# Half-row tiles for three convolutions, no copied outer rows, and two later stages further behind

## The reference

```python
x = x + L0(gn(x))   # 5 Newton-Schulz steps for the inverse of each 128x128 matrix
x = x + L1(gn(x))   # 3x3 convolution of activations rounded to whole numbers of up to 127,
                    # integer weights, scale and bias; the scale comes from the largest |gn(x)| of the batch
x = x + L2(gn(x))   # 5x5 convolution whose kernel is zero off its diagonal
x = x + L3(gn(x))   # 3x3 circular convolution (written with FFTs)
```

## Time and profile before

| | us |
|---|---|
| median of 3 runs | 4041.86 (4040.77 to 4042.82) |
| the profiled execution | 4042.99 |
| its span | 4041.2 |
| TensorE busy, VectorE busy | 3882.1, 3161.3 |
| ScalarE busy, GpSimd busy | 2458.9, 2416.6 |

### The profile page before, as it was taken

How to read it: one execution, slowest core, us unless ns; L and a number is a source line. 1 busy time by engine, 2 the same in 40 slices (tenths; PEclk the granted TensorE clock), 3 DMA queues, 4 the chain that set the end, 5 groups by cost and what they waited for, 6 DMA issues and landing times. The chain is left out here.

```text
span 4041.2 us, 91064 instructions
## 1 busy us (share of the span) xinstructions
PE 3882.1 (96%) x35017; PEld 2994.3 (74%) x35017; DVE 3161.3 (78%) x7205; ACT 2458.9 (61%) x4490; POOL 2416.6 (60%) x3154
## 2 busy tenths in 40 slices
PE   7999999999999999999999589999999999999998
PEld 7999999999999999999999344444444444444443
DVE  5888888888888888888888667777777777777774
ACT  5776677777777777777777345455455455555552
POOL 6888888888888888888888323333332332332332
PEclk9999999999999999999999799999999999999999
DMA  2122211222122222221221368777777777778774
GB/s 71 56 63 64 64 59 59 64 64 59 58 64 64 64 64 64 64 64 56 61 64 43 75 133 175 174 165 162 164 168 175 169 160 163 169 171 175 162 159 106
DMA packets 339918, 422.11 MB, mean 104 GB/s; under 512 B 25312, under 2 KB 288160, under 8 KB 323104
## 3 DMA queue, kind: packets, MB, share of 16 engines
q1 hardware_dynamic: 324128, 377.40, 39.1%
q10 hardware_dynamic: 15360, 38.88, 3.7%
HBM read 135.18 MB, written 134.22 MB: 67 GB/s over the span
## 5 line engine op out<-in xcount | busy, mean ns | idle before, releaser
L1228 POOL TENSOR_TENSOR xn<-F,xn 128x512 f16<-128x512 f32 x512 | 543.4, 1093 | 1189.6 <-ACT xn L1270 1189.6
L1444 PE MATMUL bank<-xn,wt 128*128 128x512 f16 (+1 forms) x3072 | 765.0, 384 | 15.3 <-DVE xn L1314 11.8
L484 ACT ACTIVATE P<-bank 128x512 f32<-128x512 f32 x1024 | 606.6, 608 | 267.6 <-PE bank L1007 155.4
L1466 PE MATMUL bank<-xk,wt 128*32 128x512 f16 x6144 | 634.9, 386 | 43.3 <-DMA xk<-xn 42.9
L1328 DVE SCALAR_TENSOR_TENSOR x<-bank,wu,x 128x512 f32<-128x512 f32 x512 | 377.4, 747 | 299.7 <-PE bank L1471 269.9
L1444 PEld LDWEIGHTS bank<-xn,wt 128*128 128x128 f16 (+1 forms) x3072 | 296.0, 102 | 361.8 <-issue 40.1
L1267 ACT ACTIVATE F<-x,nb,r 128x2048 f32<-128x2048 f32 x128 | 268.1, 2095 | 346.6 <-issue 218.6
L1471 PE MATMUL bank<-xk,wth 128*32 128x512 f16 x3072 | 469.2, 381 | 0.0
L1466 PEld LDWEIGHTS bank<-xk,wt 128*32 128x32 f16 x6144 | 295.6, 95 | 204.9 <-DMA xk<-xn 47.6
L334 POOL TENSOR_TENSOR W<-W 128x512 f16<-128x512 f32 x256 | 289.5, 1160 | 145.1 <-ACT W L517 145.1
L1338 DVE BATCH_NORM_STATS2 bs<-x 128x6 f32<-128x512 f32 x512 | 355.5, 694 | 17.6
(11 more groups left out here) (144 smaller groups left out, 8369.3 us busy)
## 6 DMA issues: line engine op xcount, KB each, us to landing
xk<-xn SPq DMA_DIRECT2D x512, 131.8 KB, 4.4
X<-in_x SPq DMA_DIRECT2D x64, 1024.0 KB, 4.8
x_scratch<-X SPq DMA_DIRECT2D x64, 1024.0 KB, 5.8
X<-x_scratch SPq DMA_DIRECT2D x64, 1024.0 KB, 8.6
out<-x SPq DMA_DIRECT2D x64, 1024.0 KB, 6.8
xh<-xn SPq DMA_DIRECT2D x192, 131.8 KB, 4.6
xh<-xn ACTq DMA_DIRECT2D x192, 131.8 KB, 5.5
xh<-xn SPq DMA_DIRECT2D x192, 65.9 KB, 5.2
```

Of the source, the lines that this page charges most:

```text
L484: nc.scalar.activation(into[:, 4 * q:4 * q + 4, :], banks[q][:, :].rearrange("p (m w) -> p m w", m=4), ACT.Copy).then_inc(sb, 1)
L1228: ins = nc.gpsimd.tensor_tensor(padded(xn[l][n % 2], 1)[:, a + 1:a + 5, L:L + H], F[l][:, a:a + 4, :], padded(xn[l][n % 2], 0)[:, a + 1:a ...
L1444: nc.tensor.matmul(bank, wt[l][:, a, k, :], v, start=(k == a == b == 0), stop=False)
L1466: nc.tensor.matmul(bank[32 * q:32 * q + 32, :], wt[2][:, a, e, 32 * q:32 * q + 32], rows(b, 2 * q + e, 0), start=(a == b == e == 0), stop= ...
```

## The change

- `LATE` becomes (None, 0, 2, 4): layer 2 of image `s - 2`, layer 3 of image `s - 4`; the means and variances of layer 3 are those of image `s - 3`. The pipeline has one step more. Layer 2's x has three buffers (was two).
- Every convolution is cut into strips of 64 rows by 32 columns: four strips (the column groups) on the upper 64 rows of the array, four on the lower. Outer rows are read in place: the upper half's strip of column group 0 in the band below, or the lower half's of group 3 in the band above, as the tables `back` say, with weights `wth` laid over the same partitions and columns. `xh`, its 12 DMAs an image, and ScalarE's waits for them are gone.
- TensorE's stream interleaves: after each four upper strips of one piece come four lower strips of an earlier piece, in another PSUM bank. Lower strips follow one to three pieces behind, and are brought up to date (`finish`) before a mean or variance that needs them.
- `xk` is written in two passes, high part after `high` and low part after `normed`, 16 DMAs of half the size; SyncE first waits until layer 2 of image `s - 2` is done.
- On ScalarE `wrap` comes after `upper` of layer 2. `var(2, s)` on TensorE comes after the first piece of layer 2 instead of after the last of layer 3.
- Weights: `whf[1]`, `whf[3]` become 128 x 3 x 128 (were 96 x 128), are zeroed by GpSimd and filled by 6 small DMAs each; scaling and splitting cover the larger tiles. SyncE waits for those zeros.

The core of the diff:

```diff
-        outer = (None, 6 * C, H, 6 * C)
+        edges = (None, [(row, d + 1, o) for row, d, o in HALO1], [(row, 0, o) for row, _, o in HALO2],
+                 [(row, d + 1, o) for row, d, o in HALO1])
+        planes = (None, 3, 1, 3)
...
-                    for l, rows in ((1, w1h), (3, w3h)):
-                        sp.dma_start(whf[l][:, :], rows).then_inc(w_loaded, 16)
-                    sp.wait_ge(ones_set, 4)
-                    for k, (row, _, o) in enumerate(HALO2):
-                        r = row % RB
-                        sp.dma_start(whf[2][C * r:C * r + C, C * o:C * o + C],
-                                     w2h[C * k:C * k + C, C * o:C * o + C]).then_inc(w_loaded, 16)
+                    sp.wait_ge(ones_set, 6)
+                    for l, rows in ((1, w1h), (2, w2h), (3, w3h)):
+                        for k, (row, plane, o) in enumerate(edges[l]):
+                            r = row % RB
+                            sp.dma_start(whf[l][C * r:C * r + C, plane, C * o:C * o + C],
+                                         rows[C * k:C * k + C, C * o:C * o + C]).then_inc(w_loaded, 16)
...
-            LATE = (None, 0, 1, 3)
+            GAP = BEHIND = 2
+            LATE = (None, 0, 2, 4)
...
+            products = (None, [(0, 0)], [(0, 0), (0, 1), (1, 0)], [(0, 0), (0, 1), (1, 0)])
+            length = [None] + [len(products[l]) * mats[l] for l in (1, 2, 3)]
...
-                    sp.wait_ge(normed[1], 1)
-                    halo_copies(sp, 1, 0, False)
                     sp.wait_ge(xk_zeroed, 2)
                     for s in range(STEPS):
-                        if there(s - 1):
-                            sp.wait_ge(normed[2], s)
-                            for r in range(RB):
-                                skew_row(sp, r, s - 1)
+                        two, mid, three = images_of(s)
                         if there(s + 2):
                             load(s + 2)
-                        if there(s + 1):
-                            sp.wait_ge(normed[1], s + 2)
-                            halo_copies(sp, 1, s + 1, False)
-                        if there(s - 3):
-                            store(s - 3)
-                        if there(s - 2):
-                            sp.wait_ge(wrapped, 2 * (s - 1))
-                            halo_copies(sp, 3, s - 2, False)
+                        if there(three):
+                            store(three)
+                        if there(s):
+                            need(sp, conv_ps[2], BPI * (s - 1))
+                            sp.wait_ge(high[2], s + 1)
+                            skew(s, 0)
+                            sp.wait_ge(normed[2], s + 1)
+                            skew(s, 1)
...
-                        if there(s - 2):
-                            wrap(s - 2)
-                            act.wait_ge(wrapped, 2 * (s - 1))
-                            halo_copies(act, 3, s - 2, True)
                         if there(s):
                             upper(2, s)
+                        if there(mid):
+                            wrap(mid)
...
+                    def strips(l, n, u, half, i):
+                        a, b = products[l][i // mats[l]]
+                        k = i % mats[l]
+                        if half == 0 and i == 0:
+                            if u == 0:
+                                ready(l, n)
+                            bank_free(l, n, u)
+                        bank = bank_of(l, n, u)
+                        part = slice(64 * half, 64 * half + 64)
+                        for q in range(4):
+                            back = {(1, 0): -1, (0, 3): 1}.get((half, q), 0)
+                            cols_ = slice(32 * q, 32 * q + 32)
+                            w = (wth if back else wt)[l][part, a, k, cols_]
+                            if l == 2:
+                                at = (4 * u + 1) * PW + L + SK - (2 * q + k) + back * (PW + RB)
+                                v = xk[n % 2][part, b, at:at + 4 * PW].rearrange("p (j w) -> p j w", w=PW)[:, :, 0:H]
+                            else:
+                                at = 4 * u + 1 + back
+                                v = padded(xn[l][n % 2], b)[part, at:at + 4, L + k - 1:L + k - 1 + H]
+                            ins = nc.tensor.matmul(bank[cols_, :], w, v, start=(half == i == 0),
+                                                   stop=(half == 1 and i == length[l] - 1))
...
+                    def piece(l, n, u):
+                        k = place[l, n, u]
+                        for i in range(length[l]):
+                            strips(l, n, u, 0, i)
+                            if below[0] < k - (i < GAP):
+                                lower_strips()
+                        while below[0] < k - BEHIND:
+                            lower_strips()
...
                     for s in range(STEPS):
+                        two, mid, three = images_of(s)
+                        for u in range(BPI):
+                            if there(s):
+                                piece(1, s, u)
+                        if there(mid):
+                            mean(3, mid)
+                        for u in range(BPI):
+                            if there(three):
+                                piece(3, three, u)
+                            if there(mid) and u == 0:
+                                if there(s):
+                                    finish(1, s, BPI - 2)
+                                var(3, mid)
+                            if there(s) and u == 1:
+                                mean(2, s)
+                        for u in range(BPI):
+                            if there(two):
+                                piece(2, two, u)
+                            if there(s) and u == 0:
+                                if there(three):
+                                    finish(3, three, 0)
+                                var(2, s)
+                    finish(*order[-1])
```

More of the change, by code:

```diff
@@ L1115, in conv_net @@
             THIRD = 3
-            xs = [None, x1s] + [[sb(f"x{l}_{n}", [H, NJ, H]) for n in range(k)] for l, k in ((2, 2), (3, THIRD))]
+            xs = [None, x1s] + [[sb(f"x{l}_{n}", [H, NJ, H]) for n in range(k)] for l, k in ((2, THIRD), (3, THIRD))]
             T = sb("T", [H, NJ, H])
-            xh = [None] + [None if l == 2 else [sb(f"xh{l}_{n}", [6 * C, parts[l], NJ * PW], kinds[l]) for n in range(2)]
-                           for l in (1, 2, 3)]
             xk = [sb(f"xk{n}", [H, 2, SFLAT], f16) for n in range(2)]
@@ L1141, in conv_net @@
             wrap_chain = sem("wrap_chain")
-            halo = [None] + [[sem(f"halo{l}_{n}") for n in range(2)] for l in (1, 2, 3)]
-            skewed = halo[2]
+            skewed = [sem(f"skewed{n}") for n in range(2)]
             xk_zeroed = sem("xk_zeroed")
+            upper_ps = sem("upper_ps")
             conv_ps = [None] + [sem(f"conv_ps{l}") for l in (1, 2, 3)]
@@ L1386, in _ @@
                     for s in range(STEPS):
+                        two, mid, three = images_of(s)
                         for u in range(BPI):
-                            if u == BPI - 1 and there(s - 2):
-                                deviations(3, s - 2)
+                            if u == BPI - 1 and there(mid):
+                                deviations(3, mid)
                             if there(s):
@@ L1435, in conv @@
                                 pe.wait_ge(wrapped, 2 * n + 2)
-                        bank_free(l, n, u)
-                        products = [(0, 0)] if l == 1 else [(0, 0), (0, 1), (1, 0)]
-                        for k in range(taps[l]):
-                            at = L + k - taps[l] // 2
-                            for a, b in products:
-                                v = padded(xn[l][n % 2], b)[:, 4 * u + 1:4 * u + 5, at:at + H]
-                                nc.tensor.matmul(bank, wt[l][:, a, k, :], v, start=(k == a == b == 0), stop=False)
@@ L1484, in var, with lower_strips @@
                                          stop=True).then_inc(gvar[l], 1)
-                    for s in range(STEPS):
-                        if there(s):
-                            for u in range(BPI):
-                                conv(1, s, u)
-                        if there(s - 2):
-                            mean(3, s - 2)
+                    below = [0, 0]
+                    def lower_strips():
+                        k, i = below
+                        if i == 0:
+                            pe.wait_ge(upper_ps, k + 1)
+                        strips(*order[k], 1, i)
+                        below[:] = [k, i + 1] if i + 1 < length[order[k][0]] else [k + 1, 0]
@@ new lines, in piece, with finish @@
+                    def piece(l, n, u):
[6 more added lines that the diff above has]
+                            lower_strips()
+                    def finish(l, n, u):
+                        k = place[l, n, u]
```

(4 more changed lines are left out.)

128 lines of the change are left out of this document (47 added, 81 removed).

## The result

The changed kernel takes 3908.39 us (median of 4 runs, 3891.88 to 3914.69) against 4042.34 for the kernel before: a ratio of 0.9663 (95% interval 0.9632 to 0.9693), 134 us less. The forecast was 3725. The direction came true and the time lies in the range, but less than half of the gain is there. The profiled execution took 3911.49 us, 1.8 more than its span.

What follows compares the result with a forecast made beforehand. Prediction: TensorE bounds the old kernel at 26.44 us a step; afterwards VectorE's loop does at 21.9. Ends of 2433 + 59 x 21.9 = 3725 us, range 3670 to 3990.

Steps and rivals of the forecast that it cites:

- Tiles on TensorE: TensorE's convolutions: 74 turns a step at 0.218 us, 16.1 us, with upper and lower strips running at once.
- small products: TensorE's four products for means and variances: 0.5 us each with the array emptying either side, 1.9 us a step.
- Halves take turns: Rival, 20% together with slow issue: row halves do not overlap, 144 turns, 33.3 us a step, 4398 us.
- weight loads are exposed: Rival, 6%: 0.10 us of weight load shows in each TensorE turn, 25.4 us a step, 3932 us.
- side sum: Claim that halves taking turns decides once overlap is worth less than a third of the lower strips.
- VectorE's loop: VectorE as next bound: 12.0 + 9.7 = 21.7 us a step, including a wait for ScalarE's root; bounds 21.5 to 22.6.
- keeping up: Check that the other engines are in time for VectorE; TensorE's variance of layer 2 had 1.7 us of slack.
- a - 1.4: Time 1.4 us before a, the end of VectorE's part A, when TensorE passes layer 3's variance.
- The clock: Rival, 10%: TensorE idles about 4 us a step and its clock falls; up to 1.5 us a step, 3740 to 3815.
- a pair of load and product: TensorE issue, 576 pairs an image: 35 ns each reaches the loop of 21.9 us, 43 ns is break-even.
- 17 us of cover: Skewed copies of layer 2's input land near a + 31.5, needed near a + 49, two steps on.
- The ends: Time outside the 59 full steps: 2356 us of fill plus 77 of drain, 2433 (20 either way).

Runs made afterwards that it cites:

- e6_var: Changed kernel with layer 3's variance and layer 2's mean each one piece of layer 3 later on TensorE; 3767.1 us, ratio 0.9312.
- e9_var_root: e6_var with ScalarE's root of layer 2 also put ahead of the bias; 3712.6 us, ratio 0.9186.
- e1_fill: Changed kernel plus unused TensorE products, 10 ahead of layer 3's variance and 5 ahead of its mean; 3835.5 us, ratio 0.9494.
- e5: e1_fill with each image's store cut to 1 of 16 bands, most output left out; 3809.0 us, ratio 0.9420.
- e4: Changed kernel with the old distance, layer 2 one image behind and layer 3 three; 3908.5 us, ratio 0.9675.
- e7_var_root_fill: e9_var_root plus 6 unused filler products on TensorE ahead of the mean of layer 3; 3711.3 us, ratio 0.9182.
- e11_fill_root: e1_fill with ScalarE's root of layer 2 also put ahead of the bias; 3831.1 us, ratio 0.9479.
- e2_root: Changed kernel with ScalarE's root of layer 2 ahead of the bias instead of behind it; 3916.7 us, ratio 0.9697.
- e3_turns: Changed kernel with halves not interleaved: all upper strips of a piece, then all lower strips of the piece before; 4224.3 us (1 run).

## Why the prediction was right and wrong

**Tiles on TensorE: right.** A turn of 8 strips takes 0.22 us, the halves run side by side, weight loads stay hidden. The small products came to 0.42 us each against 0.5 (0.64 us from the turn before one to the turn behind it, less a turn). *Halves take turns* and *weight loads are exposed* fell. The Trainium skill, "TensorE: Matmul & The Clock Gate", Part 3, says that a weight load overlaps matmuls in flight only where their row groups differ. The turns above disagree with it, as the earlier trace rows did: each loads weights for rows that are in use, and still takes 0.22 us. One side sum was off: by the prediction's own numbers the halves had to overlap for about four tenths of the lower strips to break even (with its ends it breaks even at a step of 27.25 us, which holds 116 of the 144 turns), not for a third. Nothing hung on it.

**VectorE's loop: right for a kernel that keeps TensorE out of the way, not for this one.** The step of 21.7, bounds 21.5 to 22.6, is what e6_var runs at (21.71 at best, 21.93 in the mean), with ScalarE's root as its wait, as the prediction had it, and e9_var_root shows that root to be the bound there.

**The step that failed** is the one on keeping up: "TensorE passes var(3) at about a - 1.4, then needs 9 + 9 + 9 + 6 turns and two small products ... Slack 1.7 us". The turns were counted right, but to the wrong point. Between layer 2's variance and its reciprocal VectorE has layer 3's last residual, and the lower strips for it come 5 turns behind the variance, 1.2 us. That residual could start only at 3075.18, and the reciprocal behind it at 3075.85, 0.57 us after the root was done (3075.28). So the slack was not 1.7 but below zero: the floor became 22.24 instead of 21.7, and what makes TensorE late, from wherever it comes, had no slack to hide in.

**Two things made it late.** (a) The clock. The rival named it and gave it 10%, with a price of up to 1.5 us a step only beyond a slack of 1.7. The fall itself is there (nearly a fifth of the steady time at half clock, as the 0.91 says), and e1_fill prices it at 1.37 us, within what the rival had allowed; the supposed slack was the error, and with it the 10%. (b) Late code packets, which the prediction did not have. It asked whether a pair of load and product costs 35 ns or more to issue; pairs went through at 27 ns (8 in a turn of 0.218 us). But the packets of 256 instructions come too late now and then, for 0.5 to 2.3 us at a time. e5 shows 0.36 us a step to be the store's doing.

**The distance.** That the skewed copies have 17 us of cover was argued for two images' distance; e4 shows that one would have done. It costs nothing in the steps (24.50 against 24.53) and 5 us in the ends (2464 against 2459).

**The ends**: 2433 was forecast, 2360.4 + 103.9 = 2464 measured. The fill was right within 4 us (2356). The drain was put at 77 us by counting TensorE's turns, and took 103.9: in it mean, layer 3, layer 2 and part C follow one another, 23 us a step, and the granted clock is 0.78. That is read from the trace; nothing was run to test it or to tell the chain from the clock.

**The sum**: 3725 to 3908 are 183 us. 31 are the ends, 59 x (22.24 - 21.9) = 20 the floor, and 59 x (24.50 - 22.24) = 133 the scatter. Of the 133, fillers give back 81 through the clock, and leaving most of the store out 21 more; some 30 stay open between the other code packets and what clock and chain do together. All 153 of the steps are gone in e6_var (59 x (24.50 - 21.93) = 152). Some of that may have come by its better clock (0.97), but e7_var_root_fill against e11_fill_root shows 1.94 us a step (23.11 to 21.17) from the moved turns at the same clock and the same `issue` waits. So the missing lead of TensorE is shown to be the cause without which the others cost little.

## What to carry to other kernels

When a change frees the engine that was the bound, follow its stream to each product that the new bound reads, not just to the first, and count the slack at the last of them. The freed engine of this kernel met idle stretches, a lower clock and late code, and needed that slack for them. Put a wait for another engine behind as much ready work as there is; one piece later was worth 141 us here, the fillers that cured the clock 73. An order that brings nothing (e2_root) can bring 54 us once the chain ahead of it is cut.

## What the runs showed of the hardware

- More instructions cost time although their issue does not. TensorE got 584 pairs of load and product through in a step of 22.24 us, but waited up to 2.3 us for code packets of 16 KB, in part because of the store (e5: 28.6 us of such waits in 1000 instead of 41.7). The kernel before, with a third of the rate, never did.
- Adding 15 products a step (3.3 us of work) made a kernel 73 us faster (e1_fill), with the clock at 1.00, the 2.4 GHz level, where it had been 0.91.
- Strips of different row halves overlapped without being interleaved in the program (e3_turns). The Trainium skill, "TensorE: Matmul & The Clock Gate", Part 3, says that matmuls start and end strictly in program order. The trace of e3 disagrees: upper strips of a later block start at 3001.40, between lower turns of the block before at 3001.38 and 3001.59.
- From 2500 to 3500 us e3_turns had a clock of 0.81 with TensorE recorded busy for 916 us, the changed kernel 0.91 with 831, the kernel before 1.00 with 965: recorded busy time is no sign of a full clock. Products that run at half clock also last longer, which fills that record.
